# Two layer norms in 64-token pieces, a router in column tiles, and an expert bias folded into the weights

## The reference

```python
x = x + conv(_ln_c(x))          # conv: instance norm (affine), q/k/v 1x1, attention in 8x8 windows
                                # with 4 heads of 8 channels, projection with bias
t = tokens(x)                   # (8, 4096, 32)
t = t + ffn(_ln_t(t))           # eps 1e-5
# ffn: p = softmax(t @ router_w + router_b) over 8 experts; the two largest, renormalised;
#      sum over those two of p_e * (t @ expert_w[e] + expert_b[e])
def _ln(v): return (v - mean(v)) / sqrt(var(v) + eps)   # over the 32 channels
```

## Time and profile before

| what | value |
|---|---|
| median of the runs | 525.16 us |
| the profiled execution's own time | 523.7 us |
| its span | 522.0 us |
| TensorE matmul, VectorE, ScalarE, GpSimd busy | 427.4, 410.2, 244.4, 79.9 us |
| mean granted TensorE clock | 0.96 |

### The profile page before, as it was taken

The page is one execution under the profiler, slowest core; times in us unless marked ns, Lnnn a source line. Parts: engine busy times, 40 slices in busy tenths (PEclk is TensorE's granted clock), DMA queues, the critical chain, the costliest instruction groups (busy, mean ns, idle before and its releaser), DMA issues.

```text
span 522.0 us, 12739 instructions
## 1 busy us (share of the span) xinstructions
PE 427.4 (82%) x4882; PEld 233.9 (45%) x4882; DVE 410.2 (79%) x575; ACT 244.4 (47%) x409; POOL 79.9 (15%) x88
## 2 busy tenths in 40 slices
PE   4796799999999999999999989746959878668773
PEld 1232266666666666666666655312424323112210
DVE  0488877888888888888889887586799899899553
ACT  2653376565665656666566567061612532112110
POOL 6810000000000000000000000000422522453532
PEclk9999899999999999999999999896999989988888
DMA  8300000000000000000000000093208536556551
GB/s 315 142 0 1 1 3 1 3 0 0 0 0 0 0 0 0 0 0 0 0 0 0 0 1 3 17 205 76 57 21 186 158 91 162 149 121 155 154 145 41
DMA packets 10901, 28.80 MB, mean 55 GB/s; under 512 B 3200, under 2 KB 4736, under 8 KB 10496
## 3 DMA queue, kind: packets, MB, share of 16 engines
q1 hardware_dynamic: 8400, 20.46, 15.4%
q0 software_dynamic: 2048, 6.29, 3.9%
q10 hardware_dynamic: 432, 1.77, 0.9%
HBM read 5.96 MB, written 4.19 MB: 19 GB/s over the span
## 4 chain that ended last, share of the span: by engine, by line
PE 51%; DVE 23%; issue 9%; ACT 6%; SPq 5%; DMA 2%; DVEq 1%; POOL 1%; ACTq 0%; POOLq 0%
PE psum L445 9%; PE psum L462 9%; PE psum L305 5%; PE psum L430 4%; PE psum L587 4%; SPq L206 4%; PE psum L406 3%; PE psum L401 3%; DVE window_work L913 3%; DVE neg_max L910 3%; PE psum L325 3%; PE psum L471 3%; PE psum L579 2%; PE psum L557 2%; DVE o_tok L921 2%
## 5 line engine op out<-in xcount | busy, mean ns | idle before, releaser
L715 ACT ACTIVATE probs<-psum 128x512 f32<-128x512 f32 x128 | 76.0, 595 | 51.2 <-PE psum L445 50.8
L445 PE MATMUL psum<-weights_sb,window_work 128*128 128x128 f32 x512 | 82.0, 283 | 4.2 <-DVE window_work L913 4.2
L913 DVE TENSOR_TENSOR window_work<-psum,neg_max 128x1024 f32<-128x1024 f32 x64 | 78.4, 1225 | 7.2
L462 PE MATMUL psum<-probs,v_cols 128*32 128x64 f32 x2048 | 82.4, 223 | 0.2 <-DVE o_tok L921 0.2
L910 DVE TENSOR_REDUCE neg_max<-psum 128x16 f32<-128x1024 f32 x64 | 77.3, 1208 | 3.1 <-PE psum L430 3.1
L445 PEld LDWEIGHTS psum<-weights_sb,window_work 128*128 128x128 f32 x512 | 58.3, 142 | 47.4 <-issue 39.6
L256 POOL TENSOR_TENSOR window_work<-stage,q_sb 128x512 f32<-128x512 f32 x16 | 20.6, 1290 | 364.1 <-ACT q_sb L806 354.5
L462 PEld LDWEIGHTS psum<-probs,v_cols 128*32 128x32 f32 x2048 | 61.7, 110 | 23.8 <-issue 20.9
L579 PE MATMUL psum<-gate_rows,gate_sel_sb 128*128 (+1 forms) x128 | 45.4, 407 | 13.1 <-DVE probs L1065 5.6
L430 PE MATMUL psum<-stage 32*64 32x256 f32 x1024 | 36.1, 389 | 15.6 <-ACT stage L699 12.8
L699 ACT ACTIVATE stage<-k_sb,weights_sb 128x512 f32<-128x512 f32 x64 | 45.7, 718 | 0.0
(11 more groups left out here) (95 smaller groups left out, 610.6 us busy)
## 6 DMA issues: line engine op xcount, KB each, us to landing
stage<-x_win SPq DMA_DIRECT2D x112, 128.0 KB, 2.6
out<-out_sb POOLq DMA_DIRECT2D x16, 256.0 KB, 2.5
stage<-in_x SPq DMA_DIRECT2D x3, 1024.0 KB, 14.3
stage<-x_win POOLq DMA_DIRECT2D x16, 128.0 KB, 3.3
gate_rows<-gate_parts SPq DMA_DIRECT2D x48, 32.0 KB, 1.8
stage<-in_x SPq DMA_DIRECT2D x2, 512.0 KB, 6.2
weights_sb<-weights ACTq DMA_DIRECT2D x1, 875.5 KB, 10.1
gate_f<-gate_sel ACTq DMA_DIRECT2D x1, 512.0 KB, 13.4
```

The lines of the kernel that those rows point to most:

```text
L445: last = nc.tensor.transpose(bank[TURN_BANKS[v % 2]][:, k * P:k * P + P], shifted[:, unit % 2 * 2 + half_b, at:at + P], const["c_ident"][: ...
L462: last = nc.tensor.matmul(bank[OUT_BANK][C * b:C * b + C, at:at + TOK], v_cols[:, u, (win * IMG + b) * HALVES + hh, :, :, :].rearrange("p ...
L715: nc.scalar.activation(probs[:, w % 4, :], bank[TURN_BANKS[w % 2]][:, :], ACT.Exp).then_inc(exp_done, 1)
L913: nc.vector.tensor_tensor(shifted_unit[:, unit % 2, :, :], t, neg_max[:, unit, :].unsqueeze(2).to_broadcast([P, 2 * PAIRS * HEADS, TOK]), ...
```

## The change

- The variances of a quad are no longer computed as 512 columns on repeated partitions. For each of 8 pieces of 64 tokens, `variances` multiplies with a shifted `mean_pieces[r]`, which puts piece r on its own partitions; the 8 pieces add up in 64 columns. So `std` and `rstd` are 128 x 64. It takes 32 matmuls of 64 columns a quad, in four column tiles.
- `spread` takes piece r of chunk j from the 32 rows of j with `spread_pieces` (built on chip at the start by `constants`): 32 matmuls of 64 columns a quad, in four row tiles, or two and two chunks in the mixture. Their results are released when all 8 pieces of a chunk are done.
- `router` multiplies the four chunks in four column tiles with one 32-column block each.
- The expert bias moves into the expert weights (`experts_sb`, built by `fold_experts`): the normalised channels sum to zero, so row 31 of each block is free to hold a one; the weights take off its row from the others and put the bias there. The token copies move 31 rows, from SP and from POOL; POOL fills `stage` with ones in two parts, when the first norm's last use of it is over and after the last scores. The `bias` matmuls and the gate step 21 go away, and GATE_OPS falls to 25.
- `q_two` and `rstd_first` get memory of their own; the loop over quads in the first norm and the one over mixtures are unrolled in TensorE's program.

```diff
-                        sp.dma_start(x_rep[32 * e:32 * e + 32, pair, b, :, :].rearrange("p j n -> p (j n)"),
-                                     t_norm[32 * b:32 * b + 32, bass.ds(at, 2 * CHUNK)]).then_inc(x_rep_in[pair], 16)
+                        sp.dma_start(x_rep[32 * e:32 * e + 31, pair, b, :, :].rearrange("p j n -> p (j n)"),
+                                     t_norm[32 * b:32 * b + 31, bass.ds(at, 2 * CHUNK)]).then_inc(x_rep_in[pair], 16)
...
             sp.wait_ge(ln2["normed"], QUAD + NORMED)
+            sp.wait_ge(filled, 5)
             repeat_tokens(first[0], 0)
+            sp.wait_ge(filled, 6)
             repeat_tokens(first[2], 1)
-            sp.wait_ge(filled, 4)
...
+            pool.wait_ge(x_win_ready, CHUNKS)
+            pool.wait_ge(ln1["centred_ps"], CHUNKS)
+            pool.memset(stage[:, 0:half], 1.0).then_inc(filled, 1)
+            pool.wait_ge(score_ps, 2 * CHUNKS)
+            pool.memset(stage[:, half:2 * half], 1.0).then_inc(filled, 1)
+            pool.wait_ge(filled, 6)
...
-                    pool.dma_start(x_rep[32 * e:32 * e + 32, 1, b, :, :].rearrange("p j n -> p (j n)"),
-                                   t_norm[32 * b:32 * b + 32, bass.ds(at, 2 * CHUNK)]).then_inc(x_rep_pool, 16)
+                    pool.dma_start(x_rep[32 * e:32 * e + 31, 1, b, :, :].rearrange("p j n -> p (j n)"),
+                                   t_norm[32 * b:32 * b + 31, bass.ds(at, 2 * CHUNK)]).then_inc(x_rep_pool, 16)
...
+            for r in pieces:
+                for j in range(QUAD):
+                    last = nc.tensor.matmul(bank[at][32 * j:32 * j + 32, 0:PIECE], mean_pieces[r],
+                                            squares[:, j, r * PIECE:r * PIECE + PIECE],
+                                            start=(r == 0), stop=(r == PIECES - 1), skip_group_check=True)
...
+        def spread(pe, sems, quad, js, banks, source, pieces=range(PIECES)):
...
+            for r in pieces:
+                for j in js:
+                    rows = slice(32 * j, 32 * j + 32)
+                    one = nc.tensor.matmul(bank[banks[j % len(banks)]][:, r * PIECE:r * PIECE + PIECE],
+                                           spread_pieces[rows, r, :], source[rows, :], start=True, stop=True)
...
             for q in range(2, QUADS):
                 pe.wait_ge(x_loaded[q], 16)
-            with pe.Fori(0, QUADS - 2) as q:
                 for j in range(QUAD):
-                    spread_first(q, j)
-                    centre(pe, ln1, q + 2, j, natural)
-                variances(pe, ln1, q + 2)
+                    centre(pe, ln1, q, j, natural)
+                    spread_first(q - 2, range(2 * j, 2 * j + 2))
+                variances(pe, ln1, q)
+            fold_experts(pe)
...
+                for j in range(QUAD):
+                    start = (quad * QUAD + j) * CHUNK
+                    one = nc.tensor.matmul(bank[2][32 * j:32 * j + 32, at], const["c_router"][:, 0, 0:C],
+                                           t_norm[:, start + at.start:start + at.stop], start=True, stop=True)
...
-                if at == 8:
-                    pe.wait_ge(gate_step, (quad - 1) * GATE_OPS + (1 + ONE))
-                    variances(pe, ln2, quad)
-                if 0 <= at - 11 < 2 * QUAD:
-                    spread(pe, ln2, quad, (at - 11) // 2, LN2_BANKS, half=(at - 11) % 2)
-                if 0 <= at - 20 < 2 * QUAD:
-                    router(quad, (at - 20) % QUAD, half=(at - 20) // QUAD)
+                if at in (8, 9):
+                    if at == 8:
+                        pe.wait_ge(gate_step, (quad - 1) * GATE_OPS + (1 + ONE))
+                    variances(pe, ln2, quad, pieces=range(4 * (at - 8), 4 * (at - 7)))
+                if 11 <= at < 19:
+                    js, part = ((0, 1), (2, 3))[(at - 11) // 4], (at - 11) % 4
+                    spread(pe, ln2, quad, js, LN2_BANKS, rstd, range(2 * part, 2 * part + 2))
+                if at in (20, 21):
+                    router(quad, half=at - 20)
...
-                        if k == 3:
-                            bias(quad, j)
```

More of the change, by code:

```diff
@@ L308, in centre, with variances @@
                 one.then_inc(sems["centred_ps"], 1)
[L310 to L321, removed]
-                pe.wait_ge(sems["rstd_ready"], quad + (1 + ONE))
[L323 to L328, removed]
+        def variances(pe, sems, quad, at=2, pieces=range(PIECES)):
+            if pieces[0] == 0:
+                pe.wait_ge(sems["std_ready"], quad + ONE)
+                pe.wait_ge(sems["squared"], quad * QUAD + (QUAD + XC))
+            for r in pieces:
[3 more added lines that the diff above has]
+                                            start=(r == 0), stop=(r == PIECES - 1), skip_group_check=True)
+            if pieces[-1] == PIECES - 1:
+                last.then_inc(sems["var_ps"], 1)
@@ L374, in _, with constants, fold_experts, spread_first @@
             pe.wait_ge(first_loaded, 16)
-            def spread_first(quad, j):
-                spread(pe, ln1, quad, j, LN1_BANKS, rhs=rstd_first[:, bass.ds(quad * CHUNK, CHUNK)])
+            def constants(pe):
+                pe.wait_ge(const_step, 2)
+                for r in range(PIECES):
+                    last = nc.tensor.matmul(bank[3 + r // 4][:, r % 4 * P:r % 4 * P + P],
+                                            ident_pad[:, PIECES - r:PIECES - r + P], spread_one[:, :],
+                                            start=True, stop=True)
+                last.then_inc(spread_ps, 1)
+            def fold_experts(pe):
+                pe.wait_ge(const_step, 7)
+                nc.tensor.matmul(bank[7][:, 2 * C:4 * C], fold[:, :], const["c_we"].rearrange("p a n -> p (a n)"),
+                                 start=True, stop=False, skip_group_check=True)
+                for eh in range(2):
+                    nc.tensor.matmul(bank[7][:, (2 + eh) * C:(3 + eh) * C],
+                                     bias_sel[:, eh, :, :].rearrange("p i c -> p (i c)"), const["c_eb"][:, 0, 0:C],
+                                     start=False, stop=(eh == 1), skip_group_check=True)
+            def spread_first(quad, pieces=range(PIECES)):
+                spread(pe, ln1, quad, range(QUAD), LN1_BANKS, rstd_first[:, quad, :], pieces)
             for q in range(2):
@@ L524, in chunk @@
                         centre(pe, ln2, 0, 3, tokens, banks=(SHARED,))
-            for j in range(QUAD):
-                spread_first(QUADS - 2, j)
+            spread_first(QUADS - 2)
             queries(0)
@@ L543, in _, with router @@
             weigh(CHUNKS - 1, 1, NW - 3)
[L544 removed]
             weigh(CHUNKS - 1, 1, NW - 2)
[L546 removed]
             weigh(CHUNKS - 1, 1, NW - 1)
[L548 to L554, removed]
+            spread(pe, ln2, 0, range(QUAD), LN2_FIRST, rstd)
+            def router(quad, half=None):
+                if half != 1:
+                    pe.wait_ge(ln2["normed"], quad * QUAD + (QUAD + NORMED))
                     pe.wait_ge(ln2["std_ready"], quad + (1 + ONE))
                 at = cols(half)
[L557 to L560 removed]
+                for j in range(QUAD):
+                    start = (quad * QUAD + j) * CHUNK
+                    one = nc.tensor.matmul(bank[2][32 * j:32 * j + 32, at], const["c_router"][:, 0, 0:C],
+                                           t_norm[:, start + at.start:start + at.stop], start=True, stop=True)
+                if half != 0:
                     one.then_inc(logits_ps, 1)
@@ L627, in mixture @@
                 experts(quad, QUAD - 1, 1)
-            for j in range(QUAD):
-                router(0, j)
+            router(0)
             project(CHUNKS - 1, at=5)
@@ L637, in _ @@
             variances(pe, ln2, 1)
-            for j in range(QUAD):
-                spread(pe, ln2, 1, j, LN2_BANKS)
-            for j in range(QUAD):
-                router(1, j)
+            for js in ((0, 1), (2, 3)):
+                spread(pe, ln2, 1, js, LN2_BANKS, rstd)
+            router(1)
             pe.wait_ge(x2_done, CHUNKS + X2)
-            with pe.Fori(0, QUADS - 2) as q:
+            for q in range(QUADS - 2):
                 mixture(q, norm_next=True)
@@ L786, in gate_copies @@
             def gate_copies(quad, step, first=False):
-                if step != 22:
-                    act.wait_ge(gate_step, quad * GATE_OPS + (step + ONE))
-                if step == 22 and not first:
+                act.wait_ge(gate_step, quad * GATE_OPS + (step + ONE))
+                if step == 21 and not first:
                     for j in range(QUAD):
@@ L829, in _ @@
             gate_exps(0)
-            for step in (21, 22, 24):
+            for step in (21, 23):
                 gate_copies(0, step, first=True)
@@ L878, in _ @@
+            constants()
             reciprocals_first(0)
```

106 lines of the change are left out of this document (76 added, 30 removed).

## The result

The changed kernel takes **950.37 us** (median of four runs, 949.93 to 952.21); the kernel before, run beside it, 524.93 (519.74 to 525.29). The ratio is 1.815, 95% interval 1.804 to 1.827: slower by four fifths. The prediction said 935, between 895 and 1400. The profiled execution's span is 948.2 us where the prediction had 932.

A forecast was written before the change was run, and what follows sets the result against it. SP's 31-row token copies, serialised on one DMA engine, were taken as the bound: 335 + 20 + 18.6 + 541 for 112 copies = 915, plus 14 other traffic and 3 cold clock, span 932; 935 us forecast, range 895 to 1400.

The forecast's parts named there:

- The forecast's mechanism: SP's token copies: 31 is prime, so each whole copy goes through one DMA engine and they serialise; chance 0.74.
- the other traffic: Gate rows, outputs and POOL's copies on the same engine: 18 us, of which 14 counted on the path.
- Start of the first copies: Second norm, quad 0 normalised: 337.0 before, first norm +1.5, second norm up to the copies -3.7, hence 335 us.
- A copy on one engine: 31 rows of 4096 bytes at 0.156 us each, uncrowded: 4.83 us a copy.
- rival 3: Token copies on one engine at the crowded price, 9.0 us a copy: about 1400 us; chance 0.06.
- Up to mixture 0: Mixture 0 needs gates, which stand behind all of the first 28 copies at 4.83 us each.
- Mixture 0's first two chunks: Start of mixture 0: some 20 us before SP may refill their buffer, read from 21.9 in mixture 2.
- The other 84 copies: After mixture 0's first chunks the engine never rests: 3 x 28 more copies at 4.83 us each.
- Tail: End of the kernel, after SP's transfers: 18.6 us left.
- Signs: Trace marks: small packets about 1520, DMA share near 0.06, clock halved, reciprocals 0.55 us, batches 2.3, loop 8.7, router 1.1.
- Rival 1: The 31 rows still spread over 16 engines, copies cost as now, the rest saves 15.3: about 510 us; chance 0.14.
- Rival 2: As Rival 1, but the norms' small load-and-multiply pairs cost 0.072 us, not 0.036: 540 us; chance 0.04.

The follow-up runs named there:

- experiments 1 and 2: Kernel before with 31-row copies: 950.41 us; with 30-row copies: 533.45. Changed kernel with 32-row copies: 532.72; with copies split 16 + 15: 584.29.
- best version: Changed norms and router, bias matmuls as before, 32-row copies, plus unread matmuls only between the stages: 516.22 us, ratio 0.9849 to the kernel before.
- unfolded version: Changed norms and router with the expert bias matmuls as before and 32-row copies: 523.19 us; with all of the added unread matmuls 519.82.

## Why the prediction was right, and where it was not

The forecast's mechanism was shown (experiments 1 and 2), with its time 15 us short of the median. Term by term (the other traffic, 14, stands with the 84 copies, and the 3 for TensorE's cold starts with the tail):

- **Start of the first copies**: 335 predicted, 335.40 measured. Two errors cancel: the first norm came out +4.1 (the first scores start at 62.27 us, before at 58.21), not +1.5. From the first queries on TensorE ran at half clock (46.32 to 62.27 us is 15.95, before 47.46 to 58.21, 10.75; with the added matmuls 47.32 to 58.71, 11.39, so that 4.6 of the 5.2 is the clock). The stretch up to the copies came out 5.7 shorter (4.1, and 1.6 for 337.04 to 335.40), not 3.7.
- **A copy on one engine**: 4.83 predicted, 4.79 measured. That nothing crowds it was right, and rival 3's 9.0 us is out.
- **Up to mixture 0**: 28 copies, 135 us by the sum; 335.40 to 475.31 is 139.9, with gate moves and the clearing of the queue: +4.7.
- **Mixture 0's first two chunks**: 20 predicted. SP refills from 501.65, 26.3 after 475.31: +6.3. The 20 came from mixture 2, which prepares no norm. Mixture 0 does, and in the kernel before it took 24.65 us from its first matmul to the refill, at full clock. So 4.7 of the 6.3 come from the row that the prediction chose; the other 1.7 came with a mean clock of 0.76 here, 0.50 from 492 to 504 us. The window of the kernel before:

```profile
366.96:391.61 24.65, 18.29 (x92) 8.28 (x91) 22.51 (x32) 11.20 (x18) 8.79 (x10) 1.00 0.13 37
```

- **The other 84 copies**: 405.7 and 14 for other traffic, 419.7. From 501.65 to the last landing at 929.1 it is 427.5: +7.8, not taken apart further. With 4.79 a copy (402) the other traffic and gaps come to 25, where 14 were counted.
- **Tail**: 18.6, and 3 for cold starts, 21.6. From 929.1 to 948.2 it is 19.1: -2.5.
- The sum of these, +0.4 + 4.7 + 6.3 + 7.8 - 2.5, is +16.7, and 932 + 16.7 is the span of 948.2 within rounding. Only the start of the copies came out right by luck; the others add up, and most are short.
- **Signs**: small packets 1536 where about 1520 was said (POOL's 16 fillings), a DMA share of 0.06 at 26 GB/s, half the clock in the pauses, reciprocals of 64 columns 0.54 us (0.55 said), a loop of 8.50 (8.7 said), a router of 1.94 at half clock (1.1 said; 1.06 where the added matmuls held the clock). Variances take 1.04 us and not 2.3: four column groups overlap better than two, as the lower bound had it. The gate moves stayed behind the copies, as said.

**Rival 1's size failed** (510 us, had the copies kept their engines), and with it the sum of the rest of the change. The step that failed is "The copies cost what they cost now, and the sum is ... -15.3". It prices every edit from rows at full clock and sets the clock's answer at nothing. Without the 31 rows, and all else as changed, the kernel stands at 532.72, 23 us above it. Rival 2 (540 us, with 0.072 us a pair) lies near that. At full clock the first norm's pairs took 0.016 and 0.031 to 0.038 us; at half clock its last spreads took 0.058 and those of the second norm 0.115. So what rival 2 feared came in part, by the clock, which it does not name. By the combines (first of mixture 0, each mixture, the last of all), that version against the kernel before:

| stretch | predicted | fold, 32 rows | best version |
|---|---|---|---|
| to the first combine (384.17 before) | -9.5 | -4.4 | -11.9 |
| mixture 0 (24.58) | -2.2 | +8.8 | +4.8 |
| to mixture 1's first combine (16.83) | in the mixtures | -2.3 | -2.7 |
| mixture 1 (24.42) | -2.2 | +8.9 | +2.3 |
| from there to the last combine (65.18) | -1.4 | -0.7 | -0.7 |

The best version keeps the bias matmuls, so the column "predicted" is not quite its own. With the clock held, the first row is what the prediction had and 2.4 more. The mixtures never are: they were forecast faster and are slower in every version. Of mixture 0's +8.8, 4.2 come back when matmuls are added, net of what these cost themselves. The mixtures' own loss beside the clock is argued and not shown apart: variances after an expert group, and spreads that VectorE waits for. The prediction's sum for a mixture (-2.8, +1.3, -0.7) has no term for the spreads at all. They took 0.074 us a pair there, where it had 0.036 for a pair and named 0.072 as a bound: in the mixture only two row groups run at a time.

## What to carry to other kernels

Before a tile copy loses a row, factor the count. In each count tried on SP's queue (15, 16, 30, 31 and 32 rows) the number of small packets fits the largest divisor up to 16: 31 rows hold one engine for 4.79 us a copy, where copies of 32 and 30 land in 2.6 and 2.5. Cutting the copy at a multiple of 16 brings the engines back, but count the issues: here two for one cost 52 us over whole copies of 32 rows (584.3 against 532.7). Two other ways were not tried: to copy the row anyway and overwrite it, and to let POOL's queue issue all of the copies.

When an edit makes TensorE's work shorter, look at the granted clock of the stretches around it. Here a forecast gain of 15 us became a loss of 8, and matmuls that nobody reads gave back 13 of these 23; in the unfolded version 19 of them gave 7. In the control on the kernel before, with its clock at 0.96, they gave nothing, and inside the mixtures of the unfolded version they gave nothing: first see that the clock was lost on the path.

## What the runs showed of the hardware that I had not expected

- A 128 KB copy over 16 engines holds SP's queue 0.592 us (median), one over 15 engines 0.800. With 56 issues at alternately 16 and 15 rows the mean is 0.75 (42.08 us).
- With copies that go to one engine, SP's queue is held for 4.79 us an issue (median of 112), after a few that take 0.6: what is queued behind them, here the gate moves, waits too.
- POOL's queue does not send 31 rows to one engine: its copies land in 2.5 us in the changed kernel and in 3.5 in the kernel before with only that edit (3.3 with 32 rows), with one small packet more a copy, and the time stays (523.49).
- Pairs of load and multiply with 64 moving columns, at full clock: 0.016 us in four column groups, 0.031 (64 on end) to 0.0375 (16) in four row groups, 0.060 (32 on end) to 0.074 (8) in two row groups.
- Less TensorE work gave a lower granted clock: 0.96, 0.911 and 0.882 as the norms and then the bias matmuls were thinned out, and 0.944 to 0.968 when work without use was put in.
